# Weights given in the order they are kept, one-hot rows for two batch tiles, and more of the last tiles' banks inside the last chunk

## The reference

```
e    = stack([tbl_f[ids[:, f]] for f in range(32)], axis=1)    # 512 x 32 x 32
cur0 = relu(einsum over (h, m) of e[b,h,d] * e[b,m,d] * filter_0[h*m, n])   # 512 x 128 x 32
cur1 = relu(einsum over (h, m) of e[b,h,d] * cur0[b,m,d] * filter_1[h*m, n])
z    = concat(cur0, cur1).sum over d                           # 512 x 256
h    = relu(concat(z, dense_ctx) @ W_top1 + b_top1)            # 272 -> 512
h    = relu(h @ W_top2 + b_top2)                               # 512 -> 256
y    = h @ W_top3                                              # 512 x 1
```

## Time and profile before

| | us |
|---|---|
| median of 3 runs | 897.17 (896.67 to 898.1) |
| the profiled execution's own time | 897.55 |
| its span in the trace | 895.4 |
| PE busy | 844.7 (94%) |
| DVE busy | 770.6 (86%) |
| ACT busy | 765.4 (85%) |
| POOL busy | 656.9 (73%) |
| first bank of layer 1 begins | 64.55 |

### The profile page before, as it was taken

How to read it: one execution, slowest core, us unless ns; L and a number is a source line. 1 busy time by engine, 2 the same in 40 slices (tenths; PEclk the granted TensorE clock), 3 DMA queues, 4 the chain that set the end, 5 groups by cost and what they waited for, 6 DMA issues and landing times.

```text
span 895.4 us, 14503 instructions
## 1 busy us (share of the span) xinstructions
PE 844.7 (94%) x3621; PEld 675.7 (75%) x3621; DVE 770.6 (86%) x2404; ACT 765.4 (85%) x2582; POOL 656.9 (73%) x623
## 2 busy tenths in 40 slices
PE   0569999999999999999999999999999999999997
PEld 0246888888877888888887888888888888888773
DVE  1435999999999999999999999998899999999774
ACT  0239999999988999999998999999999999999862
POOL 6535788887788887888888888876676666677580
PEclk9879999999999999999999999999999999999999
DMA  6537667667757676677767667667766767665430
GB/s 203 155 82 185 168 160 164 148 150 175 169 131 167 161 158 156 146 165 163 163 154 168 161 152 166 146 155 167 163 152 153 171 150 156 156 147 111 85 57 0
DMA packets 57778, 132.92 MB, mean 148 GB/s; under 512 B 8744, under 2 KB 22960, under 8 KB 57598
## 3 DMA queue, kind: packets, MB, share of 16 engines
q0 software_dynamic: 22128, 68.57, 42.3%
q1 hardware_dynamic: 34542, 60.77, 21.1%
q10 hardware_dynamic: 1024, 2.67, 0.9%
HBM read 62.35 MB, written 5.15 MB: 75 GB/s over the span
## 4 chain that ended last, share of the span: by engine, by line
PE 83%; ACT 4%; DVE 4%; issue 3%; DMA 2%; POOL 2%; another core or an unknown queue 1%; SPq 0%; DVEq 0%; POOLq 0%
PE ya L837 14%; PE ya L839 14%; PE ya L838 14%; PE yd L839 10%; PE yd L837 10%; PE yd L838 10%; PE acc L837 3%; ACT scaled L527 3%; PE acc L839 3%; PE acc L838 3%; DMA ids_across<-in_ids_first 1%; DVE acc L734 1%; DMA scaled<-scaled 1%; PE yd L971 1%; PE acc L866 1%
## 5 line engine op out<-in xcount | busy, mean ns | idle before, releaser
L527 ACT ACTIVATE scaled<-ya,emb 128x128 f32<-128x128 f32 x2312 | 662.7, 385 | 56.8 <-PE ya L839 49.0
L734 DVE SCALAR_TENSOR_TENSOR acc<-yd,emb,acc 128x128 f32<-128x128 f32 x1400 | 395.3, 344 | 5.3 <-PE yd L839 5.3
L385 POOL TENSOR_TENSOR quarter<-scaled 128x512 f32<-128x512 f32 x127 | 195.6, 1540 | 67.3 <-DMA scaled<-scaled 47.2
L837 PE MATMUL ya<-w_hi,prev_hi 128*128 128x512 f32 x578 | 229.2, 397 | 7.5 <-ACT scaled L527 4.0
L838 PE MATMUL ya<-w_lo,prev_hi 128*128 128x512 f32 x578 | 226.2, 391 | 0.0
L839 PE MATMUL ya<-w_hi,prev_lo 128*128 128x512 f32 x578 | 226.1, 391 | 0.0
L378 POOL DMA_DIRECT2D scaled<-scaled x127 | 120.2, 946 | 103.0 <-ACT scaled L527 93.9
L837 PE MATMUL yd<-w_hi,prev_hi 128*128 128x512 f32 x446 | 174.8, 392 | 0.6 <-DVE pooled_b L759 0.6
L839 PE MATMUL yd<-w_hi,prev_lo 128*128 128x512 f32 x446 | 173.6, 389 | 0.0
L838 PE MATMUL yd<-w_lo,prev_hi 128*128 128x512 f32 x446 | 173.6, 389 | 0.0
L361 POOL DMA_INDIRECT emb<-in_tbl,idx x120 | 125.8, 1048 | 31.3 <-issue 16.2
(11 more groups left out here) (120 smaller groups left out, 747.2 us busy)
## 6 DMA issues: line engine op xcount, KB each, us to landing
scaled<-scaled POOLq DMA_DIRECT2D x127, 512.0 KB, 8.4
xb<-xt_scratch SPq DMA_DIRECT2D x62, 512.0 KB
x<-xt_scratch SPq DMA_DIRECT2D x62, 192.0 KB
xm<-xt_scratch SPq DMA_DIRECT2D x30, 256.0 KB
scaled<-in_L_rec_filter SPq DMA_DIRECT2D x8, 256.0 KB
emb<-in_tbl,idx POOLq DMA_INDIRECT x120
xt_scratch<-xt_stage SPq DMA_DIRECT2D x7, 256.0 KB
w_second_index_twice<-in_L_rec_filter ACTq DMA_DIRECT2D x2, 512.0 KB
```

The lines of the kernel that those rows point to most:

```text
L385: pool.tensor_tensor(four, piece[:, 0:C], piece[:, C:2 * C], ALU.add).then_inc(quartered, 1)
L527: op = act.activation(scaled[:, tile % PR, C * j + N * i:C * j + N * (i + 1)], ya[:, n % RA, N * i:N * (i + 1)], ACT.Copy, scale=scale_of( ...
L734: dve.scalar_tensor_tensor(after, y_part, scale_of(tile, HB * j + i), before, ALU.mult, ALU.add).then_inc(chained, 1)
L837: pe.matmul(dst, v_hi, m_hi, start=start, stop=False)
```

## The change

Six edits are made together.

- The host gives filter_0 gathered into the two orders in which it is kept (`w0_first`, `w0_second`, `w0_small`) and filter_1 with the partition first. They are loaded from ACT's queue in 3 and 4 transfers, with 2 KB and 4 KB in a row per partition; the doubling goes. The identity, the halves and the dense context move from SP's queue to ACT's.
- The one-hot rows are made for batch tiles 0 and 1 (PICK_TILES = 2): `ids_across` has 2048 ids on each of 125 partitions (1000 KB), there are two `where` and two masks, 16 matmuls and 8 picks of a pair; `pick_ps` takes in the `yd` banks and acc0. The 8 small fields of tile 1 are gathered no more.
- `ctx_ps` moves to prod, xm_ps and both `ya`; PE waits there for the 4 pairs of tile 0, and before it turns the fields for all 8 pairs. POOL waits for all 8 too before its 13 gathers of tile 1.
- In the last chunk D banks come earlier: `d_banks` gives 4 a slot in slots 124 to 127 and the rest, six, in slot 128. The last three tiles (LATE = 3) add their `part` at the end of the chain instead of beginning with it. A banks of the last chunk go round three buffers, prod with the two `ya`.
- Pieces of the tower's first layer move among the D banks of slot 128 and behind them; POOL finishes tile 126 before it begins tile 127 (`sum_last`).
- The tower's second layer has q outer and t inner, and ACT makes each half of h2 as it is ready.

```diff
+    LATE = 3
+    D_LAST = 4
+    PICK_TILES = 2
...
-        ctx_ps = [yd[:, 0, :], yd[:, 1, :], yd[:, 2, :], ya[:, 0, :]]
-        tower_ps = [prod[:], xm_ps[:], ya[:, 0, :], ya[:, 1, :]]
+        tower_ps = [xm_ps[:], prod[:], ya[:, 0, :], ya[:, 1, :]]
...
+        pick_ps = [prod[:], xm_ps[:], ya[:, 0, :], ya[:, 1, :], yd[:, 0, :], yd[:, 1, :], yd[:, 2, :], acc0[:]]
+        ctx_ps = [prod[:], xm_ps[:], ya[:, 0, :], ya[:, 1, :]]
...
+        def a_bank(n):
+            if n < A_LAST:
+                return ya[:, n % RA, :]
+            at = (n - A_LAST) % (RA + 1)
+            return prod[:] if at == RA else ya[:, (A_LAST + at) % RA, :]
...
+        def d_banks(slot):
+            if slot < LAG or slot > TILES:
+                return []
+            if slot < TILES - DC:
+                return [(slot - LAG, j) for j in range(dq(slot - LAG))]
+            first = d_number(TILES - DC - LAG, 0) + D_LAST * (slot - (TILES - DC))
+            return D_BANKS[first:first + D_LAST if slot < TILES else None]
...
-            sp.dma_start(ids_across[0:PICK_P], dram(ids_first, 0, [[0, PICK_P], [1, len(SMALL) * P]])).then_inc(pick_loaded, 16)
+            sp.dma_start(ids_across[0:PICK_P], dram(ids_first, 0, [[0, PICK_P], [1, PICK_TILES * len(SMALL) * P]])).then_inc(
+                pick_loaded, 16)
...
-            for h in range(0, F, HB):
-                sp.dma_start(w1_raw[:, h:h + HB, :], dram(filter_1, h * N * N, [[N, P], [N * N, HB], [1, N]])).then_inc(
-                    w1_loaded, 16)
...
             pool.wait_ge(later_ids_loaded, 16)
-            pool.wait_ge(picked, len(PAIRS))
+            pool.wait_ge(picked, PICK_TILES * len(PAIRS))
             pool.wait_ge(gathered[0], 16 * GATHERED_LAST)
...
-            act.wait_ge(w0_doubled, 64)
+            act.dma_start(w0_a, w0_first).then_inc(w0_loaded, 16)
+            act.dma_start(w0_b, w0_second).then_inc(w0_loaded, 16)
+            act.dma_start(w16, dram(w0_small, 0, [[0, 3], [N, F], [1, N]])).then_inc(w0_loaded, 16)
...
+            for s in range(4):
+                fields = slice(s * F // 4, (s + 1) * F // 4)
+                act.dma_start(w1_raw[:, fields, :], w1[:, fields, :]).then_inc(w1_loaded, 16)
...
+            find(0)
             dve.wait_ge(ids_loaded, 16)
...
+            number_within(0)
+            dve.wait_ge(where_made, 2)
+            find(1)
...
+            dve.wait_ge(later_ids_loaded, 16)
+            number_within(1)
+            pick_rows(0)
             dve.wait_ge(w_hi_ready, 2)
...
+            pick_rows(1)
...
-                if tile == TILES - 1:
-                    dve.wait_ge(part_ready, TILES)
+                if tile >= TILES - LATE:
+                    dve.wait_ge(part_ready, tile + 1)
...
             pe.wait_ge(ctx_share_ready, H1 // P)
+            pe.wait_ge(picked, PICK_TILES * len(PAIRS))
             pe.wait_ge(four_times_ready, 2)
...
-            for t in range(H1 // P):
-                pe.wait_ge(tower_relu, t + 1)
-                for q in range(H2 // P):
+            for q in range(H2 // P):
+                for t in range(H1 // P):
+                    pe.wait_ge(tower_relu, t + 1)
```

More of the change, by code:

```diff
@@ L15, in cin_tower @@
 def cin_tower(nc, dense_ctx, ids, tables, W_top1, b_top1, W_top2, b_top2, W_top3,
-              filter_0, filter_1, eye, fold_scale, ids_first, pick, out):
+              w0_first, w0_second, w0_small, w1, eye, fold_scale, ids_first, pick, out):
     B, D_CTX = dense_ctx.shape
@@ L363, in gather @@
                     bass.IndirectOffsetOnAxis(ap=idx[:, bt, f:f + 1], axis=0)).then_inc(done, 16)
+            later = [(bt, f) for bt in range(1, BT) for f in range(F) if bt >= PICK_TILES or f not in SMALL]
             pool.wait_ge(ids_loaded, 16)
@@ L369, in _ @@
             pool.wait_ge(later_ids_loaded, 16)
-            pool.wait_ge(picked, len(PAIRS))
+            pool.wait_ge(picked, PICK_TILES * len(PAIRS))
             pool.wait_ge(gathered[0], 16 * GATHERED_LAST)
-            for f in range(EARLY_NEXT):
-                gather(1, f, gathered[1])
+            for bt, f in later[:EARLY_NEXT]:
+                gather(bt, f, gathered[bt])
             def halve(tile):
@@ L916, in _ @@
                 for q in range(DC):
-                    tile = DC * c + q - LAG
-                    if tile >= TILES:
+                    if DC * c + q > TILES:
                         break
-                    for j in range(max(aq(DC * c + q), dq(tile))):
+                    behind = d_banks(DC * c + q)
+                    for j in range(max(aq(DC * c + q), len(behind))):
                         if turning(c) and (q, j) == TURN_AT:
@@ L926, in _ @@
                             bank_a(c, q, j)
[L927 to L928 removed]
+                        if j < len(behind):
+                            bank_d(*behind[j])
+                        if (c, q, j) == (CHUNKS, 0, 1):
+                            pe.wait_ge(folded0, 2 * BT)
+                            tower_pooled0(0)
+                        if (c, q, j) == (CHUNKS, 0, 3):
+                            pe.wait_ge(a_used, a_number(CHUNKS - 1, DC - 1, aq(TILES - 1) - 1) + 1)
+                            tower_pooled0(1)
                         if (c, q, j) == (0, 1, 2):
@@ L1005 @@
     args += [given("eye", np.eye(P, dtype=np.float32)), given("fold_scale", scale),
-             given("ids_first", np.asarray(inputs["ids"])[0:P, small].T), given("pick", pick)]
+             given("ids_first", ids_first), given("pick", pick)]
     y = nc.dram_tensor("y", (inputs["ids"].shape[0], 1), F32, kind="ExternalOutput").ap()
```

200 lines of the change are left out of this document (96 added, 104 removed).

## The result

Median 890.0 us (4 runs, 888.7 to 891.36) against 897.63 for the kernel before in the same set (set 1) (4 runs, 896.67 to 898.49): ratio 0.9918, 95% interval 0.9899 to 0.9937. Forecast were 892.1 us and a range of 888.0 to 896.8. The profiled execution took 889.24 us, its span is 887.1 us (before 895.4), so 2.14 us lie outside it, as before.

The account below looks back on a forecast made before the run. PE, busy 94% of the span, was taken as the bound, so only start and end could move: start -0.4, end -3.7, tower -0.9, together -5.0 us. Profiled 897.55 becomes 892.5, the median 892.1, range 888.0 to 896.8.

Parts of the forecast that it names:

- T: Start: PE's first pick matmul, put 4.6 us later, at 30.3, as the added ids load five DMA engines.
- That is the same load: Start: ACT's queue carries 2.77 MB against 2.67 before, so nothing was added to T for it.
- First turn: Start: PE's first transposition of the fields, after all picks, forecast at 48.4 us against 48.81 before.
- First turn to first bank: Start: the way from PE's first field transposition to layer 1's first bank, kept at 15.7 us.
- The second gap: Start: an unexplained 2.08 us wait of DVE, kept within the 15.7 us; without it, -2.1 to -3.9.
- Rival A: Start: PE keeps its full clock over its rest, so the turns take 2.1 us less, 890.0; chance 0.17.
- The middle: Chunk loop: eight gathers fewer free POOL, which PE doesn't wait for; 0 us, bounds -0.5 and +0.5.
- The end: Last chunk: six D banks left instead of nine, late adds; last sum at 877.0 instead of 880.66, -3.7 us.
- D: End: a later POOL makes DVE and the `yd` buffers hold PE; -3.7 becomes -1.5, 894.3; chance 0.11.
- The tower: After the last sum: layer 2 by q leaves PE one relu to wait for, -0.9 us, bounds 0 and -1.2.
- B: Start: a gap like the 3.17 us one falls into the picks, +3.2 or +6.3, 895.3 or 898.4; chance 0.18.
- C: Start: ids_across takes twice its 11.66 us, landing at 25.0; all behind moves 7.1 us, 899.2; chance 0.07.

Follow-up runs that it names:

- one_tile: Changed kernel with one-hot rows for batch tile 0 alone (PICK_TILES = 1), 8 more gathers in the loop; 887.37 us, 0.9969 of the kernel before.
- ids128: Changed kernel with ids_across broadcast to 128 partitions instead of 125; 883.49 us, 0.9917 of the kernel before.
- spread: Changed kernel with ids_across on 128 partitions and each small table in two transfers of 112 and 13 partitions; 877.84 us, 0.9865 of the kernel before.
- before_again: The kernel before the change, unaltered, profiled a second time on another chip; 889.86 us (one run).
- spread_again: The kernel of spread, unaltered, run on another chip; 883.55 us, 0.9847 of the kernel before.
- after_third: The changed kernel, unaltered, run a third time as the measure for its set; 888.99 us, 0.9913 of the kernel before.
- gathers83: Changed kernel with eight unused gathers put back into the chunk loop, 83 as before; 892.46 us, 3.4 more than the unaltered changed kernel.
- old_last_chunk: Changed kernel with the last chunk and its tower pieces in the old order; 892.22 us, 3.2 more than the unaltered changed kernel.
- layer2_old: Changed kernel with the tower's second layer in the old order, t outside and h2 made after both steps; 891.73 us (one run).
- pooled_in_wait: Changed kernel with one tower piece moved ahead of the fifth D bank of slot 128, into PE's wait for DVE; 887.98 us (one run).

## Why the prediction was right, and where it wasn't

The measured median lies in the range, but in part by luck: the middle gave 3.1 us that were put at nothing, and the tower lost 1.0 that was counted on. Two of the prediction's own signs of being wrong in the mechanism came: the turns began after 50, and the stretch from the second chunk to the last changed by over 1 us.

**T (term +4.6 us).** T moved by 7.4. The term itself was right: from one tile's ids to two it is 4.57 us (one_tile), and five engines for 125 partitions is borne out by ids128 and spread. The rest was put at nothing with "That is the same load": one_tile, with the same ids and tables to load as before, has T 3.15 us behind before_again. ACT's queue carries the same bytes in all, but filter_1 now moves while the tables do (2.12 MB on that queue from 8 to 26 us and not 0.81); 5/16 of the difference at 112 GB/s is 3.7 us, an estimate from these rows, and no run separates it. The prediction's sentence that ids_across on 128 partitions would gain 3.2 us counts only the added half; all 1.02 MB leave the five engines, which by its own rates is 1.02/112 - 1.02/357 = 6.3 us, and ids128 has 6.75.

**First turn (48.4 forecast, 51.07).** All 2.7 are the error of T (2.9): from T to the turn it took 17.9 us, and the prediction's steps give 18.1. The picks did hide fields, sorting and context share.

**First turn to first bank (15.7 kept, 12.84).** The second gap, which I had kept, was gone, and that took 2.9 us back. It was in the bounds (-2.1 to -3.9). before_again shows that it can be absent from the unchanged kernel; that it was present in one profile made it no property of the path. The start as a whole, -0.64 against -0.4, is near by two errors that cancel. The changed kernel's later T isn't wholly the loss that it seems on such a chip: a start made earlier fell into the late releases, and of 13.6 us of T 5.4 were left in the time (spread_again).

**Clock.** Rival A wasn't it, though its number (890.0) is the measured one: the granted clock fell, and already ahead of the rest (1.00 from 43 to 46 us, 0.56 from 46 to 47.7 under the last context matmuls, 0.50 in the rest), and the turns began at the lower level. But it was back at full from 56.44 on, so chunk 0's banks ran at full pace, where before they ran at half till 70.3. The 0.9 us behind the first bank can't be put down to this. Before, the clock was 0.50 in the first 3 us of banks, and in each of the other thirteen profiles it was 1.00; yet from the first bank to `prev_hi` 1 it took 21.95 us in before_again and 22.00 in after_third, as long as the 21.91 before. Over all profiles it is 20.4 to 22.3 us, and what sets it stays open.

**The middle (0, bounds 0.5, measured -3.1).** This step failed: "free POOL, which is not what PE waits for". PE's rest of 3.7 us in 783 was read as no bound by others. Three chunks, in each of which DVE waits for `part`, are together 3.0 us longer than in the changed kernel, and gathers83 gives 3.1 us of the middle back by eight gathers alone. PE's rest is only 0.8 us in these three chunks, so the busy time hid it; a list of chunk lengths, 24.7 with a few of 26, would have shown it.

**The end (-3.7, measured -3.73).** Right in its steps: 24.6 us for the A banks (836.65 to 861.2), six D banks left, two late tiles. DVE's last two tiles took 9.09 us where 9.18 was charged. old_last_chunk gives back 3.7. D wasn't seen.

**The tower (-0.9, measured +0.07).** Layer 2 by q saved its 0.9 (layer2_old). It was lost to a term that the sum put at nothing: PE's tower pieces "come while DVE adds". PE began its last D bank only at 867.84, with 0.97 us of wait in front, and the pieces behind it, from 868.64 on, fill it until the transposition at 873.27. pooled_in_wait moves one piece and gets 0.8 us back.

**B and C.** No gap in the picks, in seven profiles of the changed kernel or a variant with that T. ids_across landed at 15.40, not 25; why it came so early no run tests.

## What to carry to other kernels

Before a transfer is made larger, look at its partitions: 125 rows cost the first matmul 14 us here over 128 and 112 + 13 (T 32.85 and 19.24 on one chip), and an issuing queue that stands still was its sign. An earlier T isn't yet time: of these 13.6 us 5.4 were left in the median. A helper engine that is 77% busy over a loop (POOL, 604 of 783 us) can still be the bound in single chunks: list their lengths before a change to its work is put at zero. And before an unknown wait in one profile is kept or dropped, take a second profile of the same kernel, on another chip: here it was 6 us, where the change made 8.

## What the runs showed of the hardware

- The same kernel took 897.63, 896.78 and 896.84 us in sets 1, 3 and 4 and 890.23 in set 2, and between the two profiles of it 6.35 of 7.6 us of span lie ahead of the first bank (64.55 against 58.20), where the first has late releases and the second none.
- One of POOL's 13 gathers took 4.98 us (the others 0.94), from 57.98 on, beside DVE's `w_lo` of 2048 columns (57.67, two in 4.47 us). The same, 4.64 to 5.84 us, is in each of the 13 profiles in which gathers and `w_lo` overlap, and in none of the gathers of the kernel before, which had ended at 55.25 with `w_lo` at 59.19. No wait of PE up to 86 us names POOL.
- Counts of finished matmuls reached DVE long after the matmuls' recorded end in three profiles (spread_again: matmuls over at 28.1, counts at 37.78 to 37.96), with the cause open.
